# Expanding the upper half of the warping path inside the walk back, with the two sides in the two column halves of TensorE

## The reference, cut to what matters

```python
def _align_one(small, large):            # small: context 512x128, large: normed x 256x128
    D = _pairwise_euclidean(small, large)
    R = _dtw_cost(D)                     # R[i,j] = D[i,j] + min(R[i-1,j], R[i,j-1], R[i-1,j-1])
    i_idx, j_idx, valid = _backtrack(R, T_small, T_large)
    contrib = small[i_idx] * valid[:, None]
    return jnp.zeros((T_large, d)).at[j_idx].add(contrib)
...
x = x + _L2_xattn_ref(ctx_1024, _layernorm(x, axis=-1))
```

## Time and profile before

| | |
|---|---|
| median of 3 runs | 1122.71 us (1119.2 to 1122.84) |
| the profiled execution's own time | 1126.61 us |
| its span in the profile | 1124.7 us |
| mean granted TensorE clock | 0.885 |
| busy: TensorE / VectorE / ScalarE | 953.6 / 687.9 / 477.2 us |

### The profile page before, as it was taken

One profiled execution on the slowest core, in us unless ns is written; L12 is line 12 of the kernel. 1 busy time (PEld: TensorE's weight loads), 2 busy tenths in 40 slices (PEclk: granted clock), 3 DMA queues, 4 the chain that ended last, 5 costly groups with the idle time before them and its releaser, 6 DMA issues. The chain is left out here.

```text
span 1124.7 us, 17437 instructions
## 1 busy us (share of the span) xinstructions
PE 953.6 (85%) x6265; PEld 595.3 (53%) x6268; DVE 687.9 (61%) x2640; ACT 477.2 (42%) x1123; POOL 2.5 (0%) x15
## 2 busy tenths in 40 slices
PE   4999999899999999998898897256961199899998
PEld 3666666655666656666555555022420073576646
DVE  3656555666656566565455516999999935545353
ACT  3655555555546465454224435311332225212450
POOL 0000000000000000000000000000000000000000
PEclk9999999999999999999679878587855599866899
DMA  8720000000000000000000000000000000000000
GB/s 240 133 56 2 1 1 1 1 1 1 1 1 1 1 1 1 1 1 1 1 1 1 2 1 2 0 1 1 1 1 0 0 2 1 0 1 1 1 1 20
DMA packets 25478, 13.64 MB, mean 12 GB/s; under 512 B 13097, under 2 KB 23729, under 8 KB 25394
## 3 DMA queue, kind: packets, MB, share of 16 engines
q1 hardware_dynamic: 25394, 12.52, 4.5%
HBM read 11.99 MB, written 0.52 MB: 11 GB/s over the span
## 5 line engine op out<-in xcount | busy, mean ns | idle before, releaser
L443 ACT ACTIVATE wide_probs<-PS,wide_nmax 128x512 f32<-128x512 f32 (+2 forms) x256 | 140.4, 557 | 47.7 <-DVE wide_nmax L368 47.7
L368 DVE TENSOR_REDUCE wide_nmax<-PS 128x2 f32<-128x1024 f32 (+2 forms) x128 | 113.6, 888 | 33.1 <-PE PS L313 23.7
L313 PE MATMUL PS<-wide_kT,wide_qT 64*128 64x512 f32 (+2 forms) x512 | 110.2, 507 | 2.1 <-ACT wide_kT L437 2.1
L326 PE MATMUL PS<-constants,wide_probs 128*128 128x128 f32 x704 | 101.3, 278 | 0.0
L291 PE MATMUL PS<-wide_pT,wide_v 128*64 128x256 f32 (+1 forms) x768 | 90.2, 370 | 0.2 <-DVE wide_v L363 0.2
L326 PEld LDWEIGHTS PS<-constants,wide_probs 128*128 128x128 f32 x704 | 78.0, 141 | 18.6 <-ACT wide_probs L443 12.0
L93 PE MATMUL PS<-constants 128*128 128x256 f32 x260 | 75.9, 427 | 7.3 <-DVEq L98 7.3
L449 ACT COPY wide_pT<-PS 128x512 f32<-128x512 f32 (+2 forms) x128 | 57.7, 451 | 45.3 <-PE PS L326 45.3
L1530 PE MATMUL PS<-w_up_or_diagonal,constants 128*128 128x512 f32 (+2 forms) x44 | 30.6, 788 | 46.0 <-DVE w_up_or_diagonal L1670 46.0
L374 DVE COPY wide_pT<-PS 128x512 f32<-128x512 f32 (+2 forms) x128 | 66.2, 517 | 2.7
L291 PEld LDWEIGHTS PS<-wide_pT,wide_v 128*64 128x64 f32 x768 | 49.7, 136 | 29.3 <-issue 10.6
(11 more groups left out here) (426 smaller groups left out, 1760.0 us busy)
## 6 DMA issues: line engine op xcount, KB each, us to landing
ctx_by_lane<-ctx_dram SPq DMA_DIRECT2D x4, 256.0 KB, 7.7
top_w<-L_ffn_W_dram SPq DMA_DIRECT2D x2, 512.0 KB
constants<-constants_dram SPq DMA_DIRECT2D x1, 679.0 KB, 5.4
x<-x_dram SPq DMA_DIRECT2D x1, 512.0 KB, 4.2
l0x_wq<-L_xattn_Wq_dram SPq DMA_DIRECT2D x1, 512.0 KB, 9.2
l0x_wk<-L_xattn_Wk_dram SPq DMA_DIRECT2D x1, 512.0 KB, 5.4
l0x_wv<-L_xattn_Wv_dram SPq DMA_DIRECT2D x1, 512.0 KB, 6.6
l0x_bv<-L_xattn_bv_dram SPq DMA_DIRECT2D x1, 512.0 KB, 5.4
```

The source lines that it names most:

```text
L313: mm = pe.matmul(PS[:, self.S[qt][h], 0:self.keys(qt)], w.qT[rows, n % 2, qt * P:qt * P + P], w.kT[rows, n % 2, 0:self.keys(qt)], start=Tr ...
L326: mm = pe.transpose(PS[:, self.T[h], kt * P:kt * P + P], w.probs[:, qt, h, kt * P:kt * P + P], ident)
L368: v.tensor_reduce(w.nmax[:, (2 * n + qt) % 4, :], PS[:, self.S[qt][0]:self.S[qt][1] + 1, 0:self.keys(qt)], AX.X, ALU.max, negate=True).the ...
L443: act.activation(w.probs[:, qt, h, 0:self.keys(qt)], PS[:, self.S[qt][h], 0:self.keys(qt)], ACT.Exp, bias=w.nmax[:, (2 * n + qt) % 4, h:h ...
```

## The change

The upper slots, 64 to 157, are transposed inside the walk back, ahead of slot 40 (`TURN_AT`). Output rows are cut in halves of 64: the half that needs slots from 64 up is multiplied by TensorE in two pieces of eight lanes, between the pieces of cells (`UPPER_AT`: after those from slot 48 and from slot 32), the other half after the walk. A product then has 64 weight columns. Side 1 and side 0 of the same batch follow each other and go to the two column halves of the array, that is to different halves of the partitions of one PSUM bank, and to different columns of it. The upper half of side 1 stands in partitions 0 to 63 and its lower half in 64 to 127, so the permutation reverses each half by itself. One group of products now ends both sides; the copy of side 1 comes after it, and the addition of side 0 waits for that copy.

```diff
+    TURN_AT, UPPER_AT = 40, (48, 32)
...
     # tensor_cells
+            if a in self.UPPER_AT:
+                self.tensor_upper(pe, self.UPPER_AT.index(a))
+
+    def expand(self, pe, p, upper):
+        M = self.H // 2
+        for b in range(B):
+            for side, context in ((1, self.ctxR), (0, self.k.ctxP)):
+                first = self.HAND * p + (M if upper else 0)
+                rows = slice(M, 2 * M) if upper != bool(side) else slice(0, M)
+                mm = pe.matmul(self.k.PS[rows, b, side * D:side * D + D], self.MT[32 * b:32 * b + 32, first:first + M, self.LANES * side + p],
+                               context[32 * b:32 * b + 32, p, :], start=(p == 0), stop=(p == self.LANES - 1))
+        return mm
+
+    def tensor_upper(self, pe, part):
+        n = self.LANES // len(self.UPPER_AT)
+        pe.wait_ge(self.mt_done, 1)
+        for p in range(n * part, n * part + n):
+            self.expand(pe, p, True)
 
     def tensor_expand(self, pe):
         pe.wait_ge(self.mt_done, 2)
-        for side, context in ((1, self.ctxR), (0, self.k.ctxP)):
-            for p in range(self.LANES):
-                first = self.HAND * p
-                for b in range(B):
-                    mm = pe.matmul(PS[:, b if side else 4 + b, 0:D], self.MT[32 * b:32 * b + 32, first:first + H, self.LANES * side + p],
-                                   context[32 * b:32 * b + 32, p, :], start=(p == 0), stop=(p == self.LANES - 1))
-            mm.then_inc(self.product, 1)
+        for p in range(self.LANES):
+            mm = self.expand(pe, p, False)
+        mm.then_inc(self.product, 1)
         pe.wait_ge(self.late_in, 1)
-        pe.matmul(PS[:, 0, :], self.k.cst[:, C_ROUND:C_ROUND + P], self.late[:, :], start=True, stop=True).then_inc(self.product, 1)
+        pe.matmul(PS[:, 6, :], self.k.cst[:, C_ROUND:C_ROUND + P], self.late[:, :], start=True, stop=True).then_inc(self.product, 1)
...
     # scalar_late
         act.wait_ge(self.product, 9)
-        act.copy(self.late[:, :].rearrange("p (b d) -> p b d", b=B), self.k.PS[:, 0:B, 0:D]).then_inc(self.late_in, 1)
+        act.copy(self.late[:, :].rearrange("p (b d) -> p b d", b=B), self.k.PS[:, 0:B, D:2 * D]).then_inc(self.late_in, 1)
...
     # vector_backward
         for s in reversed(range(SLOTS)):
+            if s == self.TURN_AT:
+                self.turn(v, self.H // 2, SLOTS)
...
     def vector_expand(self, v):
-        cuts = (self.SLOTS, 96, 0)
-        for n, (b, a) in enumerate(zip(cuts, cuts[1:])):
-            v.wait_ge(self.keyed, len(self.KEY_CUTS) - 1 + self.CELL_CUTS[::-1].index(a))
-            v.transpose(self.MT[:, a:b, :].rearrange("p s l -> p (s l)"), self.MH[:, a:b, :].rearrange("p s e -> p (s e)")).then_inc(self.mt_done, 1)
+        self.turn(v, 0, self.H // 2)
         x, PS = self.k.x, self.k.PS
+        v.wait_ge(self.late_in, 1)
+        v.tensor_tensor(x[:, 0::2, :], x[:, 0::2, :], PS[:, 0:B, 0:D], ALU.add)
         v.wait_ge(self.product, 10)
-        v.tensor_tensor(x[:, 0::2, :], x[:, 0::2, :], PS[:, 4:8, 0:D], ALU.add)
-        v.wait_ge(self.product, 11)
-        v.tensor_tensor(x[:, 1::2, :], x[:, 1::2, :], PS[:, 0, :].rearrange("p (b d) -> p b d", b=B), ALU.add)
+        v.tensor_tensor(x[:, 1::2, :], x[:, 1::2, :], PS[:, 6, :].rearrange("p (b d) -> p b d", b=B), ALU.add)
+
+    def turn(self, v, a, b):
+        v.wait_ge(self.keyed, len(self.KEY_CUTS) - 1 + self.CELL_CUTS[::-1].index(a))
+        v.transpose(self.MT[:, a:b, :].rearrange("p s l -> p (s l)"), self.MH[:, a:b, :].rearrange("p s e -> p (s e)")).then_inc(self.mt_done, 1)
...
     # constants
-    c[p, C_ROUND + 127 - p] = 1.0
+    c[p, C_ROUND + 64 * (p // 64) + 63 - p % 64] = 1.0
```

More of the change, by code:

```diff
@@ L1561, in tensor_cells @@
             pe.matmul(bank, self.scaled[:, 2, :], self.signs[:, n % 2, 1, 0:b - a, :], start=False, stop=True).then_inc(self.added, 1)
+            if a in self.UPPER_AT:
[14 more added lines that the diff above has]
+            self.expand(pe, p, True)
     def tensor_expand(self, pe):
-        PS, H = self.k.PS, self.H
+        PS = self.k.PS
         pe.wait_ge(self.mt_done, 2)
-        for side, context in ((1, self.ctxR), (0, self.k.ctxP)):
-            for p in range(self.LANES):
-                first = self.HAND * p
-                for b in range(B):
-                    mm = pe.matmul(PS[:, b if side else 4 + b, 0:D], self.MT[32 * b:32 * b + 32, first:first + H, self.LANES * side + p],
-                                   context[32 * b:32 * b + 32, p, :], start=(p == 0), stop=(p == self.LANES - 1))
-            mm.then_inc(self.product, 1)
+        for p in range(self.LANES):
+            mm = self.expand(pe, p, False)
+        mm.then_inc(self.product, 1)
         pe.wait_ge(self.late_in, 1)
-        pe.matmul(PS[:, 0, :], self.k.cst[:, C_ROUND:C_ROUND + P], self.late[:, :], start=True, stop=True).then_inc(self.product, 1)
+        pe.matmul(PS[:, 6, :], self.k.cst[:, C_ROUND:C_ROUND + P], self.late[:, :], start=True, stop=True).then_inc(self.product, 1)
     def scalar_distances(self, act):
```

## The result

| | before | changed |
|---|---|---|
| median | 1123.21 us (17 runs, 1117.7 to 1128.08) | 1114.94 us (17 runs, 1109.69 to 1119.58) |
| span of the profiled execution | 1124.7 us | 1107.7 us |
| mean granted TensorE clock | 0.885 | 0.903 |

The account below looks back on a forecast made before the run. The prediction took the exposed tail of the warping stage as the bound, its products paced at 0.22 us a round. Terms +2.2 - 7.0 + 0.8 = -4.0 us gave 1118.7 us from the median 1122.71; range 1114.5 to 1122.8.

Parts of the forecast that it names:

- What bounds it: Tail of the warping stage: 21.57 us from the last scan to the last addition, all exposed.
- The first transpose: Inside VectorE's walk back, ahead of slot 40: lengthens the walk by 3.31 us, with no wait ahead of it.
- The last cells bare: After the last scan: cells formerly covered by a transpose now exposed, +2.02 us and 0.05 for the handover.
- The lower transpose: VectorE, after the last cells: 2.29 us before the lower products can start.
- The upper products cost nothing: Two pieces of 64 source matmuls in TensorE's idle time inside the walk, delaying neither cells nor walk: cost nothing.
- The lower products: TensorE after the walk: 32 rounds of eight records at 0.22 us, 14.30 us become 7.26, -7.0 us.
- The end: Last product to last addition: copy of side 1 now bare, 2.58 us instead of 1.79, +0.8 us.
- The sum: Warping stage: +2.2 - 7.0 + 0.8 = -4.0 us.
- rival A: Lower products: rounds shorten to 0.12 us at the high clock; 5.7 us, -5.6 in all, 1117.1 us; chance 0.24.
- Rival B: Lower products: column halves take turns, rounds of 0.44 us, 14.2 us, 1125.7 us (long version 1135.7); chance 0.08.
- rival C: End of the walk: upper pieces or the turn disturb walk or cells, losing up to 2 us, 1120.7 us; chance 0.06.
- the side to which I gave 0.25: Whole kernel: faster by more than 0.5% (5.6 us), under 1117.1 us; chance 0.25.

Follow-up runs that it names:

- experiment 1: Kernel before with only the transposes moved (slots 64 to 157 ahead of slot 40, 0 to 63 at the end), products unchanged: 1121.40 us, ratio 0.9988.
- experiment 6: Changed kernel with filler products (2, 3, 4 and 3) keeping TensorE busy behind the last four pieces of cells: 1116.62 us, ratio 0.9956.
- experiment 7: Kernel before with the turned path laid out so a product's 128 weight columns are neighbours, the transposes writing with a step: 1120.96 us, ratio 0.9971.
- experiment 3: Changed kernel with all of side 1, then all of side 0, within each piece, so neighbours share a column half: 1122.37 us, ratio 1.0008 against before.
- experiment 2: Kernel before with the change's products, all 512 records behind the walk, transposes as before: 1117.39 us, ratio 0.9938.
- the first interval: First comparison of the change with the kernel before, 17 runs each: ratio 0.9925 [0.9907, 0.9944].
- Experiment 4: Changed kernel with slots 8 to 63 turned under the last cells, slots 0 to 7 after, lanes 0 to 3 multiplied last: 1112.51 us, ratio 0.99 against before.
- the repeats of the change: The changed kernel run twice more, unchanged, against the kernel before: 1113.99 us, ratio 0.9933, and 1115.56 us, ratio 0.9943.
- Experiment 8: Experiment 4 with filler products (2, 3, 4 and 1) keeping TensorE busy beforehand: 1110.35 us, ratio 0.9885 against before.

## Why the prediction was right, and what was sized wrong

The measured 1114.94 us lies in the range, near its lower end, 3.8 under the forecast. By its working:

- **What bounds it.** Right. The tail was exposed: what went from the tail, less what came into the walk, is the change of the stage (-8.45 + 3.10 = -5.35).
- **The first transpose**, +3.31 forecast: it took 3.29 and the walk grew by 3.10. That the wait ahead of it is free: right, no idle time.
- **The last cells bare**, +2.02 and 0.05: 2.06. The lower transpose, 2.29: 2.31. The products started 4.42 us behind the last scan, forecast 2.07 + 2.33 = 4.40.
- **The upper products cost nothing.** Right for the cells and the walk: 868.3 to 872.1 and 875.0 to 878.5, both before the next signs (873.11 and 881.91). The clock, which in the kernel before and in experiment 1 stayed at 0.50 from the walk to the products, was at 1.00 behind each piece in this profile (872.3 to 875.7 and 879.1 to 882.5), but back at 0.50 when the lower products began.
- **The lower products**, 7.26 us and -7.0 forecast: 6.17, so **-8.1. This is the term that was mis-sized.** The step was the choice of 0.22 us for a round at both clocks. At the low clock it is 0.21, near what was said. At the high clock it is 0.125 (16 ns a record, experiment 6), the bound from below that the working had found in L1515 and not taken. My reason against it was that no stretch of the trace had records closer than 30 ns. That only told what those rows had been asked to do. By the rule of the Trainium skill on the spacing of matmul starts (TensorE: Matmul & The Clock Gate, Part 1), quoted in the prediction, 256 records could not take less than 6.4 us, an estimate from its 25 ns; they took 6.17, and in experiment 6 244 took 3.8. What bounds the round at 0.125 no run shows.
- **The end**, 2.58: 2.53.
- **The sum** for the stage, -4.0: -5.3. That is rival A, which said 5.7 us for the products and -5.6 in all. Its clock rose 3.5 us into them, the real one 4.5 us. Its mechanism has two parts. That the step in the load bounds the high clock is shown by experiment 7 (187 against 308 ns, 3.7 against 7.1 us for 128 records). That fewer columns free it is shown by experiment 3 at the high clock (26 ns a record against 54). The load record itself is not halved: from 895 to 903 in experiment 2, all at the high clock, it is 192 ns on average.

```profile
L1571 PEld LDWEIGHTS PS<-w_context_turned_round,w_path_turned 32*64 32x64 f32 x165 | 5.7, 192 | 0.0
```

Rival A had a chance of 0.24 and in hindsight deserved more than the forecast. One reading behind it was incomplete: L757's are not the only other long loads at the high clock. L1213's of `l3x_k` last 302 to 328 ns at both clocks; they too read with a step, of four, which speaks for A as well.
- **Rival B** fell with experiment 3, **rival C** with the walk and the cells above.
- **Beyond the stage** the sum had nothing. The stage gives 5.3 us (0.47%) of the 8.3. The measured gain passes 0.5%, the side to which I gave 0.25: all of the first interval lies below 0.9944. Where the other 3 us come from is open; the stages around this one, the same code, differ by more than that from profile to profile, and experiment 2 gained 7.0 us with a stage only 1.1 us shorter. That the time fell into the range is thus in part luck: the range reached that far down because of A and the spread of the runs, and A itself gave 1117.1.

Experiment 4 is the better version: its stage is 2.8 us shorter than that of the change. Against before both its comparisons exceed 0.5% (0.99 [0.9869, 0.9931] and 0.9895 [0.985, 0.9939]). Against the change its medians are 1 to 3 us lower, which the intervals do not separate; in the profile of its second comparison one later stage took 101.4 us where it took 95.0 in the repeats of the change. Experiment 8 (0.9885) is not told apart from it either.

## What to carry to other kernels

When a chain on one engine leaves another idle, put the products whose inputs are final into those gaps, and order what remains so that the data which come last are used last. Small-K products gain from column halves only if neighbours alternate between them. Work out the pace of a line at both clocks apart, and when the term that bounds it is halved, take the next bound from what is physically left (here the load of half the columns), not from the closest spacing that the old trace happens to show.

## What the runs showed of the hardware that was not expected

- Product records of 32 rows by 64 columns followed each other every 16 ns at the high clock (244 in 3.8 us), each with a weight load of its own.
- An f32 weight load of 128 columns whose elements stand 32 apart takes 308 ns at the high clock, one without a step 187. At the low clock the first takes 305 and the second 328, so the step costs nothing there. A VectorE transpose that writes with a step takes 1.93 ns an element (5933 / 3072) where the contiguous one takes 1.10 (3377 / 3072).
- Column halves of one row group overlap: 27 ns a record alternating, 52 ns one side after the other, at the low clock; 16 and 26 ns at the high one.
- TensorE at this pace outran its instructions: its loads stopped for 0.8, 1.6 and 1.0 us with nothing waited for, and each stop ended 1.3 to 1.4 us after a packet of the instruction queue had ended. The supply as its cause is inferred.
- Filling TensorE in the gaps raised the clock, but it fell again before or soon after the products began in two runs of three, and where it held, the stop above took back 1.0 of the 1.6 us that the clock was worth.
